# Two waits on GpSimd around the third tile's gather

## What is computed

```python
h = rmsnorm(layernorm(x)) * gamma
q, kv, a = split(h @ w_qkva.T)            # 256 columns each
y = associative_scan(sigmoid(a), kv)      # along the 1024 tokens
x = x + q * y
n = layernorm(x)
dispatch, combine = gating_top2(softmax(n @ router), capacity=256)   # 8 experts, 8 groups
hidden = gelu(expert_inputs @ w0) * (expert_inputs @ w1)             # H = 1368
x = x + combine(hidden @ wo)
```

## Time and profile before

| | us |
|---|---|
| median of 3 timed runs | 1648.45 |
| lowest and highest of them | 1641.49, 1649.46 |
| the profiled execution, its own time | 1658.51 |
| the profiled execution, span of its instructions | 1656.8 |

### The profile page before, as it was taken

The page is one execution under the profiler, slowest core; times in us unless marked ns, Lnnn a source line. Parts: engine busy times, 40 slices in busy tenths (PEclk is TensorE's granted clock), DMA queues, the critical chain, the costliest instruction groups (busy, mean ns, idle before and its releaser), DMA issues.

```text
span 1656.8 us, 22948 instructions
## 1 busy us (share of the span) xinstructions
PE 1620.5 (98%) x8450; PEld 1396.0 (84%) x8450; DVE 939.8 (57%) x1955; ACT 762.3 (46%) x1389; POOL 506.1 (31%) x433
## 2 busy tenths in 40 slices
PE   7999899799999999999999999999999999999998
PEld 6888788688888888888888888888888888888887
DVE  7999754345644564447544654466445644475453
ACT  5777545234433453336333543345334533453333
POOL 2156566563222222222222222222222222222211
PEclk9999999899999999999999999999999999999999
DMA  7553121025422342225211522243223422351211
GB/s 169 160 160 122 53 80 45 13 41 120 86 38 37 81 93 37 39 43 124 39 36 36 135 38 39 39 109 71 39 39 82 93 36 38 64 109 33 36 13 13
DMA packets 193848, 110.94 MB, mean 67 GB/s; under 512 B 96008, under 2 KB 189640, under 8 KB 193736
## 3 DMA queue, kind: packets, MB, share of 16 engines
q1 hardware_dynamic: 165064, 75.37, 18.1%
q0 software_dynamic: 28672, 34.10, 12.8%
HBM read 60.11 MB, written 34.61 MB: 57 GB/s over the span
## 4 chain that ended last, share of the span: by engine, by line
PE 79%; DVE 6%; issue 4%; ACT 3%; SPq 3%; POOL 2%; DMA 2%; another core or an unknown queue 1%; POOLq 0%; ACTq 0%; DVEq 0%
PE bank L1691 23%; PE bank L1714 21%; PE bank L1730 14%; PE bank L1732 8%; PE bank L1503 7%; DVE y L1440 2%; PE bank L1556 1%; PE bank L1705 1%; SPq L509 1%; ACT hhi L922 1%; DVE hlo L1443 1%; SPq L426 1%; POOL slots L658 1%; POOL out L726 1%
## 5 line engine op out<-in xcount | busy, mean ns | idle before, releaser
L726 POOL DMA_INDIRECT out<-xring,slot_records x128 | 215.4, 1683 | 858.1 <-DVE xring L1410 792.9
L922 ACT ACTIVATE hhi<-y 128x512 fp32r<-128x512 f32 (+1 forms) x349 | 220.8, 633 | 508.7 <-DVE y L1440 427.6
L1730 PE MATMUL bank<-wo,hhi 128*128 128x512 f32 (+1 forms) x1276 | 443.7, 385 | 2.0 <-DVE hlo L1443 1.8
L1440 DVE TENSOR_TENSOR y<-bank,sig 128x512 f32<-128x512 f32 x320 | 220.9, 690 | 334.1 <-PE bank L1714 300.8
L1732 PE MATMUL bank<-wo,hlo 128*128 128x256 f32 x1396 | 382.2, 274 | 0.1
L1443 DVE TENSOR_TENSOR hlo<-y,hhi 128x512 fp32r<-128x512 f32 (+1 forms) x349 | 241.6, 692 | 243.9 <-ACT hhi L922 237.6
L912 ACT ACTIVATE sig<-bank 128x512 f32<-128x512 f32 x320 | 189.6, 593 | 209.2 <-PE bank L1691 181.9
L1730 PEld LDWEIGHTS bank<-wo,hhi 128*128 128x128 f32 (+1 forms) x1276 | 239.1, 187 | 50.5 <-DVE hlo L1443 4.0
L1732 PEld LDWEIGHTS bank<-wo,hlo 128*128 128x128 f32 x1396 | 261.6, 187 | 9.2 <-issue 0.8
L1691 PE MATMUL bank<-xThi,whi 128*128 128x512 f32 (+1 forms) x704 | 217.0, 389 | 7.4 <-issue 3.5
L1691 PE MATMUL bank<-xTlo,whi 128*128 128x512 f32 (+1 forms) x704 | 213.2, 383 | 0.0
(11 more groups left out here) (147 smaller groups left out, 1730.6 us busy)
## 6 DMA issues: line engine op xcount, KB each, us to landing
stage<-in_L_ffn_w_kernel SPq DMA_DIRECT2D x160, 128.0 KB
rows<-rows SPq DMA_DIRECT2D x448, 32.0 KB, 1.9
stage<-in_L_ffn_wo_kernel SPq DMA_DIRECT2D x80, 128.0 KB
xring<-in_L_attn_x SPq DMA_DIRECT2D x16, 512.0 KB
out<-xring SPq DMA_DIRECT2D x16, 512.0 KB
x_rows<-rows SPq DMA_DIRECT2D x16, 512.0 KB
slots<-records,sloti POOLq DMA_INDIRECT x128
rows<-x_rows,slot_records POOLq DMA_INDIRECT x128
```

The costliest lines, as they stand in the source:

```text
L726: pool.indirect_dma_start(out_rows, bass.IndirectOffsetOnAxis(idx, 0), ysb[:, t % 2, j, :], None, compute_op=ALU.add).then_inc(added, 16)
L922: act.activation(h_high(e, t, hc)[0:n, :], hf[0:n, hc % 2, :], ACT.Copy).then_inc(h_hi, 1)
L1440: dve.tensor_tensor(hf[0:n, hc % 2, :], up_value(e, t, hc)[0:n, :], gel[0:n, hc % 2, :], ALU.mult).then_inc(mul_done, 1)
L1730: pe.matmul(lines(yb[j][:, :]), high, lines(wo[0:n, hc, :, :].rearrange("p s c -> p (s c)")), start=hc == 0, stop=end, skip_group_check=True)
```

## The change

Ahead of the gather of tile 2, GpSimd waits until both scatters of block 49 have landed. Behind it, it waits until the gather's four DMAs have landed, ahead of the scatters of block 50 on (the buffer's semaphore counts 64 for each gather into it, and the gather of tile 0 was the first). Nothing else differs.

```diff
--- before.py
+++ after.py
@@ -735,7 +735,11 @@
                     if (e, t) == (0, 0):
                         scatter(late, late + 2)
                     if t + 2 < FT:
+                        if (e, t) == (0, 0):
+                            landed(late + 1)
                         gather(e, t + 2)
+                        if (e, t) == (0, 0):
+                            pool.wait_ge(rows_loaded[0], 16 * FJ * 2)
                     elif not last:
                         gather(e + 1, t + 2 - FT)
                     if (e, t) == (0, 0):
```

## The result

The change made the kernel slower by about 4 us. The median of twelve runs is 1649.62 us (1646.0 to 1651.36), that of twelve runs of the kernel before beside them 1645.69 (1641.49 to 1651.17): a ratio of 1.0025 (95% interval 1.0014 to 1.0035). The forecast was 1642.9. The profiled execution moved the other way, from 1658.51 to 1650.84 us.

What follows compares the result with a forecast made beforehand. The prediction took TensorE, busy 98% of the span, as the bound: 13.7 us of stall cured, less 6.2 us waiting for rows and 2.0 us at lower clock, saves 5.5 us, giving 1642.9 us (range 1637 to 1652.5).

Steps and rivals of the forecast that it cites:

- the 13.7 us: TensorE time read as lost in three expert-loop chunks from 289.07 us, beside ScalarE stalls; the forecast had the waits end it.
- The 9.65 us of cover: GpSimd's idle time before group 7's first scatter, waiting for VectorE's records; claimed to hide the added 2.89 us.
- Rival three: Timed runs lack the stall, which may come with profiling; the waits' 2.89 us lie bare on the path: 1651.3 us, chance 0.19.
- The wait ahead of the gather: On GpSimd before the third tile's gather, for block 49's scatters: gather expected to start 1.09 us later.
- The wait behind: On GpSimd after the third tile's gather: 3.05 us from its last instruction to the next scatter, which starts 2.89 us later.
- The cured case: Stall gone, GpSimd becomes the later engine; TensorE waits 6.2 us for the fourth tile's rows: 5.5 us saved.
- The 2.0 us: TensorE's expected loss at the lower clock after its wait for the fourth tile's rows.
- Rival one: The waits change nothing: the stall returns at the same size and the waits vanish in idle time; 1648.4 us, chance 0.24.
- Rival two: The stall is cured and GpSimd is not the later engine, so all 13.7 us are saved: 1634.7 us, chance 0.08.
- Rival four: The stall moves to where GpSimd has no slack, such as the fourth tile's gather: about 1660 us, chance 0.07.
- it may be the fetch of instructions: Tentative cause of ScalarE's unexplained waits near the first three gathers, 2.97 to 7.94 us: instruction fetches held up.
- The rule to wait late: Skill rule to wait on a DMA's semaphore behind other work; by it the added GpSimd waits can only cost.

Runs made afterwards that it cites:

- late_before: Kernel before with the fourth tile's transposes moved from chunks 5 and 7 to chunks 7 and 9: 1644.87 us, ratio 1.0007.
- after_again: The changed kernel, unaltered, timed again beside the kernel before on a chip without the stall: 1647.94 against 1643.92 us, ratio 1.0026.
- after_third: The changed kernel, unaltered, timed a third time on another chip without the stall: 1648.71 against 1644.6 us, ratio 1.0034.
- ahead_only: Kernel before with only the wait ahead of the third tile's gather added, on a chip with the stall: 1652.18 us, ratio 0.9972.
- behind_only: Kernel before with only the wait behind the third tile's gather added, on a chip with the stall: 1651.51 us, ratio 0.9973.
- nopause_after: Changed kernel with the landing waits within the scatters of blocks 52 to 63 removed, on a chip with the stall: 1684.57 us, ratio 1.0145.
- after_delay: Changed kernel plus four 1 us GpSimd operations behind the second wait, on a chip with the stall: 1659.2 us, ratio 1.0018 to the kernel before.
- late_after: Changed kernel with the fourth tile's transposes moved from chunks 5 and 7 to chunks 7 and 9: 1650.9 us, ratio 1.0042.

## Why the prediction was wrong, step by step

**The failed step is the first one: the 13.7 us were read as a part of the time to be forecast.** As readings they were right: the three chunks that take 27.08 us from 289.07 on the earlier trace rows take 13.65 in the changed kernel (282.60 to 296.25), 13.4 less. But they were readings of an execution of 1658.51 us, which lies above every one of the twelve timed runs of the kernel before (highest 1651.17), and lay above the three that were known then (highest 1649.46). The prediction noted the 10 us and then set the sum 5.5 us below the median, as if the median had the stall in it. Without it the same working has nothing to save, only the waits to pay.

**The 9.65 us of cover** fell with it. They are VectorE's lateness, and VectorE was late by the stall. Rival three stated the point from which it decides: the records ready before 310.9. In `late_before` they are ready at 297.74, and GpSimd is there at 309.83.

**The wait ahead of the gather**, 1.09 us expected, is 1.10. **The wait behind** was mis-sized. It was taken as 3.05 us from the last gather instruction, from the second tile, where a small operation of 1 us lies in it; the remark in brackets guessed that the bare landing would be less. It is more: 4.07 us in this kernel, so 2.82 us were added and not 1.80. In `after_again` the idle time before the same scatter is 3.10, in `after_third` 3.29.

**The cured case** was worked out well, for a case that was half real. GpSimd became the later engine, TensorE's wait for the fourth tile's rows is 7.40 us (6.2 expected), and the clock is lower behind it: 0.50 of full speed, the 1.2 GHz level, at 340 to 345, and 0.83 at 345 to 350. The 2.0 us put down for that are right too: against the same chunks in the kernel before, TensorE loses 9.4 us there, 7.4 of them in the wait. That the wait itself came out near is in part luck. TensorE was ready for the rows at 335.48 and not at 341.5, and had them at 342.88 and not at 347.7, both some 5 to 6 us early, since the earlier stalls were missing as well; for the same reason the third gather starts at 281.94, not near 288.4. The profiled time fell by 7.67 us (1658.51 to 1650.84), which was more than the 5.5. But that compares an execution with the stall with one without it, and the gain isn't the change's alone.

**Rival three was right, at 0.19.** Its named test was that the profiled time falls and the timed median rises by some 3 us; it rose by 3.9 beside the kernel before. Its mechanism (2.89 us bare, 1651.3) is the true one with 1.0 us too little, and it gave 1651.3 where 1649.62 was measured because of its base: 1648.45 was a median of three, and of twelve it is 1645.69. What it gave as the reason, profiling, is wrong.

**Rival one** had said that the stall would not care for the waits. `ahead_only` and `behind_only` rule that out on the chip that has it: each takes one of the two stalls away and gains 0.27%. **Rival two** needed GpSimd to be early; it came to group 7 at 309.10, for records made at 298.36. **Rival four**, the stall in another place, was seen in no run with the waits unless pauses were taken out elsewhere (`nopause_after`). Only one other run with both waits was on a chip with the stall, `after_delay`.

**The step "it may be the fetch of instructions" fails for most of the stalls.** The traces record the packets of the two instruction queues, q8 and q14. If an engine stood for a fetch, a packet would come before it goes on. In the two windows of the longest stall, `nopause_after` from 329.7 to 348.2 us, and of the second stall of the kernel before, 301.5 to 309.5 us, the DMA view lists these queues and no others:

```profile
q0 software_dynamic: 432, 0.43, 9.3%
q1 hardware_dynamic: 144, 0.02, 0.6%
```

```profile
q0 software_dynamic: 172, 0.02, 2.4%
```

No instruction packet moved in either. Of the 32 waits in the table above, 25 have none in them. The seven others are the first behind the third gather; in the kernel before it has a packet of each queue between 293 and 296 us, so for these a fetch isn't ruled out. For a transfer in the way there is little either: in `nopause_after` the DMA share was 0.03 from 335 to 340 us, where three engines did nothing. The Trainium skill, in "DMA: Bandwidth & Descriptors", section "Queues, rings and completion order", says that a DMA engine takes turns between its queues packet by packet; the prediction drew from it that a fetch is never long behind a gather and that the stall has another cause. That the stall has another cause holds for the stalls without a packet; the rule itself no run here tests, since at a share of 0.03 there was hardly anything to take turns with. What the runs show is the tie to GpSimd's unbroken runs of indirect DMAs: with pauses after every four only the second stall of a long run was seen, and the first stall is longer behind twelve or sixteen than behind eight. How GpSimd holds the others up is not shown, nor why some chips don't have it.

**The rule to wait late** (the Trainium skill, "DMA: Bandwidth & Descriptors", section "Rules for kernel authors") was cited for the slower side. On chips without the stall the runs agree with it, 1.0025 to 1.0034. On a chip with it they differ: the early wait of `ahead_only` gives 0.9972 and that of `behind_only` 0.9973, and there the measurement decides. Both waits together were not timed there.

## What to carry to other kernels

Compare the profiled execution's own time with the timed runs before a stall is priced; if it lies above all of them, the stall may be none that the timed runs have, and what stands behind the stall as cover (an engine that waits 9.65 us) goes with it. A wait on an in-order engine costs nothing only as long as another releaser is later than it, so follow its path to every place where the engine that bounds the kernel is reached: here there were three, and hiding the first alone gained nothing. Where GpSimd issues many indirect DMAs, leave the pauses in that split them into short runs, and put them where the path has room; that is worth something on the chips with the stall alone.

## What the runs showed of the hardware

The same kernel differs by 0.7 to 0.95% from chip to chip (1643.92 and 1644.6 against 1656.36 and 1659.51), more than the change is worth. On one chip of the slower kind either half of the change is a gain of 4 to 5 us; on the faster ones the two together cost 4 us.

On the slower chips an unbroken run of GpSimd's indirect DMAs holds ScalarE up, for 3.0 to 6.0 us with eight in a row, 6.6 to 8.0 with twelve and 18.45 us with 28. In 25 of 32 such waits no instruction packet moves. With 28, TensorE, VectorE and ScalarE show no work at all from 335 to 345 us, while the DMA engines are at 0.03 to 0.12.

Landing is not one number. The four DMAs of a gather had landed 2.08 us after the end of the last instruction in `behind_only` (on a chip with the stall), 3.13 in the changed kernel and 3.38 in `late_after` (on chips without it). A scatter's wait for a landing is 1.39 us as a rule, and 1.91 to 2.52 at group 7's first scatter in the six runs with pauses added on chips without the stall, the changed kernel among them.
